# An audio tower's convolution stage: half-empty weight places as pairs over 64 rows, and the first norm's statistics on ScalarE

## The reference, cut to what matters

```python
# x (16, 64, 2048), conv_in_w (128, 64, 7), dw_w (128, 1, 5), pw_w (128, 128, 1)
h = conv1d(x, conv_in_w, stride=1, pad=3)
h = gelu(groupnorm1(h, gn1_w, gn1_b))            # mean and variance over channels and time
h = conv1d(h, dw_w, stride=2, pad=2, groups=128) + dw_b
h = conv1d(h, pw_w)
h = gelu(groupnorm1(h, gn2_w, gn2_b))
```

## Time and profile before

| | |
|---|---|
| time before, median of 3 runs | 2875.26 us (2874.75 to 2880.97) |
| time of the profiled execution | 2880.92 us |
| its span, first to last instruction | 2879.2 us |
| convolution stage in it | from 14.0 us (first matmul) to about 305 us |
| TensorE busy over the span | 95% |

### The profile page before, as it was taken

How to read it: one execution, slowest core, us unless ns; L and a number is a source line. 1 busy time by engine, 2 the same in 40 slices (tenths; PEclk the granted TensorE clock), 3 DMA queues, 4 the chain that set the end, 5 groups by cost and what they waited for, 6 DMA issues and landing times. The chain is left out here.

```text
span 2879.2 us, 37181 instructions
## 1 busy us (share of the span) xinstructions
PE 2728.6 (95%) x13162; PEld 2269.5 (79%) x13162; DVE 1802.0 (63%) x3214; ACT 980.1 (34%) x2012; POOL 109.0 (4%) x65
## 2 busy tenths in 40 slices
PE   7994799999999999999999999999999988979999
PEld 6772688888878888887888888788888876768888
DVE  4887576666766666677766666776666656742221
ACT  3552333333333333334233333433333333532121
POOL 2110000000000000000000000000000000211110
PEclk9997899999999999999999999999999989979999
DMA  5330232222222322222222222222222213000000
GB/s 111 73 73 0 84 95 87 80 77 76 81 73 74 95 93 81 80 81 66 82 75 79 91 92 87 67 80 81 80 80 73 95 44 155 1 16 30 22 29 30
DMA packets 55325, 206.67 MB, mean 72 GB/s; under 512 B 6768, under 2 KB 7152, under 8 KB 53168
## 3 DMA queue, kind: packets, MB, share of 16 engines
q1 hardware_dynamic: 55216, 205.26, 23.2%
HBM read 196.85 MB, written 8.39 MB: 71 GB/s over the span
## 5 line engine op out<-in xcount | busy, mean ns | idle before, releaser
L1013 PE MATMUL at_proj<-qr_xhi,at_whi 128*128 128x512 f32 x1536 | 615.0, 400 | 13.2 <-DVE at_wlo L884 8.9
L1015 PE MATMUL at_proj<-qr_xhi,at_wlo 128*128 128x512 f32 x1536 | 601.2, 391 | 0.0
L1014 PE MATMUL at_proj<-qr_xlo,at_whi 128*128 128x512 f32 x1536 | 599.6, 390 | 0.0
L754 ACT CAST at_ohi<-at_ov 128x512 fp32r<-128x512 f32 x128 | 75.0, 586 | 843.6 <-PE at_ov L1042 843.6
L1013 PEld LDWEIGHTS at_proj<-qr_xhi,at_whi 128*128 128x128 f32 x1536 | 289.4, 188 | 70.1 <-DVE at_wlo L884 9.5
L1015 PEld LDWEIGHTS at_proj<-qr_xhi,at_wlo 128*128 128x128 f32 x1536 | 289.0, 188 | 63.4
L1014 PEld LDWEIGHTS at_proj<-qr_xlo,at_whi 128*128 128x128 f32 x1536 | 289.8, 189 | 56.6
L1060 PE MATMUL at_out<-at_wohi,at_ohi 128*128 128x512 f32 x1008 | 311.5, 390 | 4.0 <-DVE at_wolo L889 3.0
L1060 PE MATMUL at_out<-at_wohi,at_olo 128*128 128x512 f32 x1008 | 311.3, 390 | 0.0
L1060 PE MATMUL at_out<-at_wolo,at_ohi 128*128 128x512 f32 x1008 | 311.2, 390 | 0.0
L896 DVE TENSOR_TENSOR h<-h,at_out 128x1024 f32 (+1 forms) x126 | 152.8, 1213 | 209.9 <-PE at_out L1060 209.9
(11 more groups left out here) (248 smaller groups left out, 4064.6 us busy)
## 6 DMA issues: line engine op xcount, KB each, us to landing
at_wstage<-in_w_qkv_dram SPq DMA_DIRECT2D x192, 512.0 KB, 3.5
at_ostage<-in_w_o_dram SPq DMA_DIRECT2D x128, 512.0 KB, 4.4
cv_x<-in_x_dram SPq DMA_DIRECT2D x32, 512.0 KB, 6.6
out_dram<-h SPq DMA_DIRECT2D x16, 512.0 KB, 2.6
fn_w_lo_raw<-in_w_t_dram SPq DMA_DIRECT2D x8, 512.0 KB, 8.6
fn_qka_lo_raw<-in_qka_t_dram SPq DMA_DIRECT2D x5, 512.0 KB, 11.2
fn_w_lo_raw<-in_dft_fwd_dram SPq DMA_DIRECT2D x4, 512.0 KB, 7.9
mx_ar<-in_a_route_dram SPq DMA_DIRECT2D x1, 544.0 KB, 4.2
```

The source lines that it names most:

```text
L1013: pe.matmul(proj[:, j % 2, :], hi[:, w], x_hi[:, k, :], start=(k == 0), stop=False)
L1014: pe.matmul(proj[:, j % 2, :], hi[:, w], x_lo[:, k, :], start=False, stop=False)
L1015: last = pe.matmul(proj[:, j % 2, :], lo[:, w], x_hi[:, k, :], start=False, stop=(k == KT - 1))
```

## The change

Three things change in `conv_stage`.

1. **Pairs over 64 rows.** The half-empty places are no longer multiplied with all 128 rows. For chunks 0 and 1 the three full places come first (`even_steps`, 9 matmuls), then three pairs (`half_slots`): a matmul over rows 0 to 63 into chunk `c`, and one over rows 64 to 127 into chunk `c + 2`. Chunks 2 and 3 then need their three full places alone (`odd_steps`, 9 matmuls).
2. **Statistics of the first norm on ScalarE.** The evacuation becomes an activation that also sums its rows. `moments` then makes minus the mean, squares the 2048 columns around it with a sum, and writes mean and variance into `mv`. VectorE loses `head(0)`.
3. **Order on ScalarE.** From step 2 on, the split of batch `it + 1` comes after the first gelu and tap 0 instead of at the head of the step. GpSimd's split of the same batch waits for it.

Besides, ScalarE waits once for VectorE's clearing of `mv` at the start.

```diff
+                act.wait_ge(cleared, 1)
...
-                    act.copy(raw[par][:, r, :], cp[:, 2 * r:2 * r + 2, :].rearrange("p a n -> p (a n)"))\
-                       .then_inc(raw_done, 1)
+                    act.activation(raw[par][:, r, :], cp[:, 2 * r:2 * r + 2, :].rearrange("p a n -> p (a n)"),
+                                   ACT.Identity, accum_out=sums[:, r:r + 1]).then_inc(raw_done, 1)
+
+                def moments(it, par):
+                    act.wait_ge(raw_done, it * 2 + 2)
+                    act.activation(halves[:, :], sums[:, :], ACT.Identity, scale=-1.0 / T_IN,
+                                   accum_out=minus_mean[:, :]).then_inc(summed, 1)
+                    act.wait_ge(summed, it * 3 + 1)
+                    act.activation(centred[:, :, :], raw[par][:, :, :], ACT.Square, bias=minus_mean[:, :],
+                                   accum_out=around[:, :]).then_inc(summed, 1)
+                    if not early(it, 1):
+                        act.wait_ge(chain, (it - 1) * CHAIN_LINKS + MIDDLE_LINKS)
+                    act.activation(mv[:, 0, 0:1], minus_mean[:, :], ACT.Identity, scale=-1.0).then_inc(summed, 1)
+                    act.wait_ge(summed, it * 3 + 3)
+                    act.activation(mv[:, 0, 1:2], around[:, :], ACT.Identity, scale=1.0 / T_IN).then_inc(head_done[0], 1)
...
-                    if on(-1):
+                    if on(-1) and early(it, 2):
                         split_in(it + 1, 1 - par)
...
+                    if on(-1) and not early(it, 2):
+                        split_in(it + 1, 1 - par)
                     if on(0):
                         evacuate(it, par, 0)
                         evacuate(it, par, 1)
+                        moments(it, par)
...
-                    if on(1):
-                        head(0, it - 1, [raw[1 - par][:, c // 2, c % 2 * BANK:(c % 2 + 1) * BANK] for c in range(NCH)])
                     if on(3):
                         dve.wait_ge(pw_done, it - 2)
-                        head(1, it - 3, [pp[:, c, :] for c in range(2)])
+                        head(it - 3)
...
+                def even_steps(i, par, c):
                     if not early(i, 1):
-                        pe.wait_ge(raw_done, (i - 1) * 2 + r + 1)
+                        pe.wait_ge(raw_done, (i - 1) * 2 + 1)
                     if c == 0:
                         pe.wait_ge(xhi_done, i + 1)
+                    first = True
+                    for weight, xs in products(i, par):
+                        if c == 0 and xs is x_lo[par]:
+                            pe.wait_ge(xlo_done, i + 1)
+                        for s in range(PAIRS - 1):
+                            w, cols = slots(c, s)
+                            pe.matmul(cp[:, c, :], weight[:, w], xs[:, cols], start=first, stop=False)
+                            first = False
+
+                def half_slots(i, par, c):
+                    if not early(i, 1):
+                        pe.wait_ge(raw_done, (i - 1) * 2 + 2)
+                    for n, (weight, xs) in enumerate(products(i, par)):
+                        w, cols = slots(c, PAIRS - 1)
+                        last = pe.matmul(cp[:, c, :], weight[HEADS_ONLY, w], xs[HEADS_ONLY, cols], start=False,
+                                         stop=(n == 2))
+                        if n == 2:
+                            last.then_inc(conv_done, 1)
+                        w, cols = slots(c + 2, 0)
+                        pe.matmul(cp[:, c + 2, :], weight[TAILS_ONLY, w], xs[TAILS_ONLY, cols], start=(n == 0),
+                                  stop=False)
+
+                def odd_steps(i, par, c):
+                    for n, (weight, xs) in enumerate(products(i, par)):
+                        for s in range(1, PAIRS):
+                            w, cols = slots(c, s)
+                            last = pe.matmul(cp[:, c, :], weight[:, w], xs[:, cols], start=False,
+                                             stop=(n == 2 and s == PAIRS - 1))
                     last.then_inc(conv_done, 1)
...
-                            pe.wait_ge(head_done[0], it * HEAD_LINKS)
+                            pe.wait_ge(head_done[0], it)
```

More of the change, by code:

```diff
@@ L251, in conv_stage @@
         dummy = sb("cv_dummy", [P, 1])
-        st = [sb(f"cv_st{n}", [P, 4, 6]) for n in range(2)]
+        st = sb("cv_st", [P, 2, 6])
+        centred = sb("cv_centred", [P, 2, T2])
+        sums, halves = sb("cv_sums", [P, 2]), sb("cv_halves", [P, 2])
+        minus_mean, around = sb("cv_minus_mean", [P, 1]), sb("cv_around", [P, 1])
         mv = sb("cv_mv", [P, 2, 2])
@@ L265, in conv_stage @@
         conv_done, raw_done = sem("cv_conv_done"), sem("cv_raw_done")
-        head_done = [sem(f"cv_head_done{n}") for n in range(2)]
+        cleared = sem("cv_cleared")
+        summed, head_done = sem("cv_summed"), [sem(f"cv_head_done{n}") for n in range(2)]
         chain = sem("cv_chain")
@@ L411, in _, with head @@
                 dve.tensor_tensor(cw_lo[:, :], cw[:, :], cw_hi[:, :].bitcast(F32), ALU.subtract).then_inc(w_lo_done, 1)
-                dve.memset(mv[:, :, :], 0.0)
+                dve.memset(mv[:, :, :], 0.0).then_inc(cleared, 1)
                 dve.wait_ge(rest_loaded, 48)
[L417 to L423, removed]
+                def head(i):
+                    link = Links(dve, head_done[1], i * HEAD_LINKS)
+                    for c in range(2):
+                        last = dve.bn_stats(st[:, c, :], pp[:, c, :])
                     link(last)
                     dve.memset(dummy[:, :], 0.0)
-                    link(dve.bn_aggr(mv[:, n, :], st[n][:, 0:len(chunks), :]))
+                    link(dve.bn_aggr(mv[:, 1, :], st[:, :, :]))
                     assert link.n == HEAD_LINKS
@@ L498, in _, with products, slots @@
                 pe.wait_ge(w_lo_done, 1)
-                def conv(i, par, c):
-                    r, at = c // 2, c % 2 * BANK
+                HEADS_ONLY, TAILS_ONLY = slice(0, C_IN), slice(C_IN, P)
+                def products(i, par):
+                    return ((cw_hi, x_hi[par]), (cw_lo, x_hi[par]), (cw_hi, x_lo[par]))
+                def slots(c, s):
+                    w = (c // 2 * PAIRS + s) * P
+                    at = c % 2 * BANK + s
+                    return slice(w, w + P), slice(at, at + BANK)
@@ L546, in body @@
                     if on(0):
-                        conv(it, par, 0)
-                        conv(it, par, 1)
+                        for c in range(2):
+                            even_steps(it, par, c)
+                            half_slots(it, par, c)
                     if on(3):
@@ L555, in body @@
                     if on(0):
-                        conv(it, par, 2)
+                        odd_steps(it, par, 2)
                     average(it, on, 0)
                     if on(0):
-                        conv(it, par, 3)
+                        odd_steps(it, par, 3)
                     average(it, on, 1)
```

## The result

| | before | after |
|---|---|---|
| median of the runs compared | 2875.38 us (4 runs) | 2911.64 us (4 runs, 2906.05 to 2913.04) |
| ratio, 95% interval | | 1.0115 (1.010 to 1.013) |
| profiled execution, its span | 2880.92, 2879.2 us | 2911.46, 2909.7 us |
| last `tail` of the convolution starts at | 291.86 us | 324.62 us |
| first projection matmul of attention | 312.34 us | 343.79 us |

The forecast was 2906, between 2888 and 2923. The medians differ by 36 us (their own ratio is 1.0126), the ratio in the table makes it 33, and the two profiled executions differ by 30.5; the one of before was near the upper end of its runs. All of it is lost in the convolution stage: from the first projection matmul to the end the kernel after is 0.9 us shorter.

The account below looks back on a forecast made before the run. TensorE bounds the whole kernel and steps 0 and 1, a loop of waits the steady convolution steps. Start steps -1.0, held taps 27.3 and clock 5 make 31 us: 2906 us, range 2888 to 2923.

Parts of the forecast that it names:

- The moved split against the taps: Steps 2 to 14: GpSimd's later split holds a VectorE tap, 2.1 us a step, 13 times, 27.3 us lost.
- the gap between taps 1 and 2: VectorE's 0.04 us between tap 1's end (133.86) and tap 2's start (133.90); GpSimd, asking at 133.4, was to win it.
- the earlier trace: Profile rows from a later stage: a 16-column VectorE operation took 1.12 us beside GpSimd's 1.30 us operation, 0.17 alone.
- The longer pause: TensorE ahead of `average` 1: pause of 2.9 us a step, clock may fall; 5 us lost, bounds 0 to 13.
- The statistics on ScalarE: First norm's sums moved off VectorE: gain 0 in steady steps; 3.5 to 4.1 us more ScalarE work, covered, cost 0.
- Cover enough: Claim that ScalarE's 3.64 us wait for the coefficients hides its added work; without it up to 1 us a step.
- The pairs: Convolution matmuls over half rows: 1.4 - x us gained in each of steps 0 and 1, 1.0 together; steady steps 0.
- x: Time the pairs of chunks 0 and 1 add ahead of the pointwise matmul: taken as 0.9 us, between 0 and 2.8.
- The sum: Whole kernel: start steps -1.0, held taps 27.3 and clock 5 make 31 us more, median 2906 us.
- The spread of the forecast: Range of the main forecast, given 78 in 100: 2893 (1.7 x 13, start gaining fully) to 2920 us.
- What would have shown it wrong: Signs in the changed profile: taps staying at 1.28 us, pair starts 0.5 us apart, ScalarE no longer awaiting the coefficients.
- The step of about 16.6 us: Predicted sign in the changed profile: a convolution step takes about 16.6 us instead of 14.55.

Follow-up runs that it names:

- e2: The kernel before with the moved split alone: from step 2 on ScalarE's split comes behind tap 0; 2905.58 us, ratio 1.0097.
- e4: The changed kernel with eleven matmuls into an unread spare bank filling TensorE's pause ahead of `average` 1; 2902.31 us, ratio 1.0083.
- e3: The changed kernel with GpSimd's subtraction issued twice a step from batch 3 on, with the same result; 2942.89 us, ratio 1.0224.
- e1: The changed kernel with ScalarE's split put back at the head of the step, pairs and statistics staying as changed; 2878.85 us, ratio 1.000.
- e8: The changed kernel with a one-column gelu at the very start, so its table loads early; 2907.79 us in one run, 2878.62 before beside it.
- e5: The kernel before with the pairs over 64 rows alone, statistics and split as they were; 2877.65 us, ratio 0.9993.
- e7: The changed kernel with the split put back, tap 4 moved behind the next `tail` and GpSimd's subtraction waiting for it; 2871.11 us, ratio 0.9968.

## Why the prediction was right, step by step

**The moved split against the taps** was the term that decides, and it held with its mechanism and nearly its size, and with its place where the clock holds. 13 steps were said, 13 have a held tap. 3.4 us were said for it: 3.33 where nothing else is late. GpSimd was said to win the gap between taps 1 and 2. It did in all 13 steps of e2 and e4, and tap 1 kept its 1.28 us. After the change it did in six; in the other seven VectorE comes later to its taps, GpSimd is in ahead of tap 1, and tap 1 is held, twice by 2.0 to 2.1 us and five times by 0.6 to 1.0.

The prediction read this gap from the earlier trace rows, which are a weak sign for it: the 1.30 us of GpSimd's operation there are hardly more than the 1.26 to 1.28 us of the seven others of its line, so a wait for VectorE can't be told in it; and these rows show an overlap at one end only, not at either. The lines quoted above show both. In numbers, tap 2 ended 1.07 us behind the end of the subtraction (151.81 and 150.74), so 0.21 us of its own 1.28 lay beside GpSimd, and GpSimd's 2.42 began 0.12 us ahead of tap 1's end: 0.33 us of overlap where 0.27 were taken. The price of the part alone is 26.2 us (e2) against 27.3. That the long operation of the earlier trace rows was on 16 columns and the taps on 1024 made no difference: what is waited for is nearly the length of GpSimd's operation. The rule of the Trainium skill that the prediction weighed there (SBUF — State Buffer, section SBUF: two separate sides), that whoever comes second waits for a whole instruction, agrees with e3 but for its edges: behind the first subtraction, which does not wait, tap 1, the second subtraction and tap 2 each wait for the one ahead, with the 0.1 to 0.2 us of overlap given above. Who comes second is not to be read from the records' starts alone (tap 1 stands 0.04 us ahead of the subtraction that holds it).

**The longer pause** was said to be 2.9 us in every step and to cost 5. It was 2.58 to 3.04 us in 8 of 13 steps and 1.24 to 1.57 in the other five; all 8 long ones were followed by a stretch of 3.4 or 6.8 us at 0.50, none of the five was. Why not in every step is something that the sum did not have: after a fall the matmuls are late, so the next pause can be short and the clock stays. After the four falls of 6.8 us it was short each time, after the four of 3.4 us once. VectorE's timeline shows such a step, behind the fall at 118.5 us:

```profile
130.30 1.29 DVE L443 BATCH_NORM_STATS2 cv_st<-cv_pp 128x6 f32<-128x512 f32 x2 [5.83 <-PE cv_pp L588]
...
131.88 1.92 DVE L482 SCALAR_TENSOR_TENSOR cv_y<-cv_g,cv_dww,cv_tap 128x1024 f32<-128x1024 f32 x1
133.84 1.28 DVE L482 SCALAR_TENSOR_TENSOR cv_y<-cv_g,cv_dww,cv_y 128x1024 f32<-128x1024 f32 x1
```

The pointwise matmul comes 2.4 us later than in the step quoted above (5.83 against 3.42 us of waiting). Meanwhile GpSimd has begun (130.28), so tap 1 is held, for 0.64 us only. The clock puts its own delay in the place of most of GpSimd's, and the step is 0.6 to 0.9 us longer than in e4. The total, 6.2 by the traces and some 9 by the medians, lies within the bounds of 0 to 13; the 5 was a choice between them, and that it came near is in part luck.

**The statistics on ScalarE** were set to 0. In the steady steps this held (wait for the coefficients 3.66 us, as before; 1.72 in e1). It failed in step 2, the term that was mis-sized: "Cover enough" was read off a steady step, and in step 2 ScalarE has neither that wait nor the last gelu, but a table load. It cost 1.86 us, once; e8 gave 1.40 of it back. That VectorE's `head(0)` is worth nothing was right: 3.42 us of waiting stand where 2.47 us of work and 0.77 of waiting stood.

**The pairs.** From the first half of a step, x was taken as 0.9 us, between 0 and 2.8. Measured it is 0.65: 6.07 us from the first matmul of chunk 0 to the last pair's start (136.53 to 142.60) against 5.42 before. The two halves of a pair run truly together: starts at most 0.01 us apart, and the next pair 0.23 us later, a matmul's pace. So the second weight load, from which I had worked out 0.9, costs nothing, and that 0.65 lies near 0.9 is luck; what costs is each change to half rows (0.34 us from the last full matmul's start to the first pair, instead of 0.23), the second pair (0.33), and the way back (0.31): some 0.3 us for each of two chunks. The rule of the Trainium skill (TensorEngine Tiling (Array Packing), section Key Properties) that a change of the mode drains TensorE agrees in sign; the pairs' starts put the price at about 0.1 us a change. The steady steps were said to gain nothing from pairs; e5 shows it (14.22 and 14.88 us).

**The sum** was -1.0 + 27.3 + 5 = 31 us. (The spread of the forecast starts, by the terms that it names, 1.7 x 13 less 2.8, at 2895 and not at 2893; the range is not touched by that.) By the profiled executions it is 30.5, made of -0.65, 25.3 for the taps, 6.2 for the clock, 1.8 for step 2, 0.1 for the last steps and some -2.3 behind the stage, which no step of mine explains. By the medians it is 36 us; the difference lies within the spread of the runs (2906.05 to 2913.04 after, 2874.75 to 2880.97 before).

**What would have shown it wrong** did not come: no step from 2 to 14 has all its taps at 1.28 us, no pair had starts 0.5 us apart, ScalarE still waited for the coefficients. The step of about 16.6 us came as 16.2 and 16.8 by turns with the clock at 1.00 throughout (e4), and as 16.2 to 17.7 after the change.

## What to carry to other kernels

An operation that is moved off one engine's busy place meets another there: look up which of its new neighbours reads two tensors in SBUF while GpSimd works, and price the meeting with nearly GpSimd's whole length (2.08 of 2.42 us here), for every turn of the loop. Work taken off an engine that then waits for something else gives nothing by itself; a new order that fills the wait can gain, as e7 does. Cover read from a steady step doesn't hold for the first turns of a pipeline, where other things, such as a table load, stand in the same place.

## What the runs showed of the hardware that I had not expected

Two matmuls over rows 0 to 63 and 64 to 127 with different weights and different target banks run as one: starts 0.01 us apart and one pair every 0.23 us, with about 0.1 us lost at each of the first pair, the second and the return. A subtraction of GpSimd that waits for a tap of VectorE is on record from its issue, so that its own length grows too (2.42 to 2.79, 2.95 and 3.27 us), while one that gets in first keeps 2.43. An operation of VectorE with one input in PSUM passed beside GpSimd where the next one, with two in SBUF, was held (e3). TensorE's granted clock fell to 0.50 after each of the pauses of 2.55 us and more ahead of `average` 1 in steps 2 to 14 (eight after the change, 13 in e3, ten in e8), after the one of 1.97 us in e1 and the one of 2.01 us in e7, after one of twelve of 1.28 to 1.78 us in e2 (1.34 us, at 131.75), and after none of eight of 1.24 to 1.63 us (five after the change, three in e8). And a kernel with 11 matmuls more in each of 14 steps (e4) was faster than the one with the pauses.
